# Twelve matmuls of a split-precision projection in another order: high by high, then the weight's low part, then the data's low part

## The reference

```python
qkv = x @ Wqkv + bqkv                      # 512 -> 3 * 512, split into q, k, v, 16 heads of 32
q_prime = exp(q @ omega - 0.5 * sum(q * q))    # 128 features a head; k_prime likewise
k_sum = sum over n of k_prime;  k_v = sum over n of k_prime (x) v
out = (q_prime @ k_v) / (q_prime @ k_sum + 1e-6)
x = layernorm(x + out @ Wout + bout)
x = layernorm(x + x @ weight.T + pooled(x) @ disha)
```

## Time and profile before

| | |
|---|---|
| runs, median (lowest to highest) | 2587.18 us (2584.82 to 2590.24), 3 runs |
| the profiled execution | 2590.89 us |
| its span | 2589.1 us |
| mean granted TensorE clock | 0.986 |
| busy: PE, PEld, DVE | 2439.8 us (94%), 1401.2 us (54%), 2010.7 us (78%) |
| busy: ACT, POOL | 1114.3 us (43%), 508.8 us (20%) |
| chain that ended last | PE 86%, DVE 7%, issue 2%, SPq 2%, ACT 2%, DMA 1% |

### The profile page before, as it was taken

One profiled execution on the slowest core, in us unless ns is written; L12 is line 12 of the kernel. 1 busy time (PEld: TensorE's weight loads), 2 busy tenths in 40 slices (PEclk: granted clock), 3 DMA queues, 4 the chain that ended last, 5 costly groups with the idle time before them and its releaser, 6 DMA issues.

```text
span 2589.1 us, 60402 instructions
## 1 busy us (share of the span) xinstructions
PE 2439.8 (94%) x24576; PEld 1401.2 (54%) x24576; DVE 2010.7 (78%) x3966; ACT 1114.3 (43%) x1921; POOL 508.8 (20%) x522
## 2 busy tenths in 40 slices
PE   5888999999999999999999999999999999987766
PEld 2445555555555555555555555555555555553333
DVE  5546878888888888888788888888888887876675
ACT  1444444444444444444445444444544444442221
POOL 2011121222212122221222222112222212211121
PEclk9999999999999999999999999999999999999998
DMA  5232233233223323322332333233223323312220
GB/s 168 67 83 56 87 92 94 67 93 100 73 81 92 95 70 95 96 75 79 96 91 76 87 96 83 71 100 88 78 85 96 92 64 99 88 54 58 58 58 33
DMA packets 158947, 214.49 MB, mean 83 GB/s; under 512 B 19312, under 2 KB 119760, under 8 KB 154448
## 3 DMA queue, kind: packets, MB, share of 16 engines
q1 hardware_dynamic: 158672, 210.63, 29.3%
HBM read 74.24 MB, written 33.55 MB: 42 GB/s over the span
## 4 chain that ended last, share of the span: by engine, by line
PE 86%; DVE 7%; issue 2%; SPq 2%; ACT 2%; DMA 1%; POOL 0%; DVEq 0%; POOLq 0%; ACTq 0%
PE bank_y L381 24%; PE bank_a L381 23%; PE bank_x L381 13%; PE bank_qf L464 4%; PE bank_kf L420 4%; PE bank_x L493 4%; PE kv_ps L438 2%; PE kv_ps L443 2%; PE bank_nm L482 2%; PE bank_nm L481 2%; PE bank_nm L480 2%; PE kv_ps L441 2%; DVE k_feat_lo L675 1%; SPq L304 1%; PE bank_x L391 1%
## 5 line engine op out<-in xcount | busy, mean ns | idle before, releaser
L792 POOL TENSOR_TENSOR rstd<-mean_var,minus_half 128x1 f32<-128x1 f32 x256 | 166.6, 651 | 1773.4 <-DVE mean_var L630 1773.4
L549 ACT ACTIVATE k_feat<-bank_kf 128x512 f32<-128x512 f32 x512 | 305.7, 597 | 232.5 <-PE bank_kf L420 220.9
L675 DVE TENSOR_TENSOR k_feat_lo<-k_feat 128x512 bf16<-128x512 f32 x512 | 358.5, 705 | 39.1 <-ACT k_feat L549 35.9
L558 ACT ACTIVATE q_feat<-bank_qf 128x512 f32<-128x512 f32 x512 | 305.5, 597 | 168.4 <-PE bank_qf L464 141.2
L682 DVE TENSOR_TENSOR q_feat_lo<-q_feat 128x512 bf16<-128x512 f32 x512 | 350.5, 694 | 33.1 <-ACT q_feat L558 29.9
L564 ACT ACTIVATE at_hi<-bank_x 128x512 f16<-128x512 f32 x128 | 76.4, 597 | 396.7 <-PE bank_x L493 396.7
L438 PE MATMUL kv_ps<-v_hi,k_feat 128*128 128x33 f16 x2048 | 208.8, 179 | 12.9 <-DVE k_feat_lo L675 9.0
L420 PE MATMUL bank_kf<-omega_s,stack_k 98*128 98x128 f16 x2048 | 199.9, 220 | 17.5 <-ACT k_feat L549 8.8
L464 PE MATMUL bank_qf<-stack_q,omega_s 98*128 98x256 f16 x1024 | 197.3, 274 | 15.2 <-ACT q_feat L558 15.2
L381 PE MATMUL bank_y<-wffn_hi,yt_hi 128*128 128x512 f16 x512 | 195.8, 382 | 16.2 <-DVE yt_lo L730 14.5
L381 PE MATMUL bank_y<-wout_hi,at_hi 128*128 128x512 f16 x512 | 195.6, 382 | 16.2 <-DVE at_lo L726 12.5
(11 more groups left out here) (118 smaller groups left out, 6076.2 us busy)
## 6 DMA issues: line engine op xcount, KB each, us to landing
xt_f<-xt SPq DMA_DIRECT2D x33, 1024.0 KB, 5.2
stack_k<-t_hi_k SPq DMA_DIRECT2D x256, 128.0 KB, 2.4
stack_q<-t_hi_q SPq DMA_DIRECT2D x256, 128.0 KB, 2.4
rows<-x SPq DMA_DIRECT2D x128, 256.0 KB, 2.9
out<-rows SPq DMA_DIRECT2D x128, 256.0 KB, 2.1
stack_k<-t_lo_k SPq DMA_DIRECT2D x128, 128.0 KB, 2.4
stack_q<-t_lo_q SPq DMA_DIRECT2D x128, 128.0 KB, 2.4
q_feat<-wqkv SPq DMA_DIRECT2D x2, 768.0 KB, 5.0
```

Of the source, the lines that this page charges most:

```text
L549: nc.scalar.activation(k_feat[:, i % 2, :], bank_kf[:, :], ACT.Exp, scale=1.0 / WS).then_inc(S["k_exp"], 1)
L558: nc.scalar.activation(q_feat[:, 2 * pair:2 * pair + 2, :], bank_qf[:, :].rearrange("p (e n) -> p e n", e=2), ACT.Exp, scale=1.0 / WS).the ...
L675: v.tensor_tensor(k_feat_lo[:, u, :], k_feat[:, u, :], k_feat_hi[:, u, :], ALU.subtract).then_inc(S["kfl"], 1)
```

## The change

`twelve` issues its matmuls by product and no longer by block: four high by high, four with the weight's low part, four with the data's low part. The halves are still six and six. The wait for the data's low part leaves the first half and stands at the ninth matmul (n == 8, the third of the last half). What KP0, WO and FF wait for in the first half is now the high part. VP, QP and the other KP had no such wait, and have one now at the ninth matmul.

```diff
-            def twelve(bank, parts, what, done):
-                at = [(kb, s, m) for kb in range(KB) for s, m in (("hi", "hi"), ("lo", "hi"), ("hi", "lo"))]
+            def twelve(bank, parts, what, done, order, low):
+                at = [(kb, *order[m]) for m in range(3) for kb in range(KB)]
                 for n in (range(0, 6) if what == "first" else range(6, 12)):
+                    if n == 8:
+                        wait(pe, *low)
                     lhs, rhs = parts(*at[n])
                     last = nc.tensor.matmul(bank[:, :], lhs, rhs, start=n == 0, stop=n == 11)
...
+            LHS_LOW_LAST = (("hi", "hi"), ("hi", "lo"), ("lo", "hi"))
+            RHS_LOW_LAST = (("hi", "hi"), ("lo", "hi"), ("hi", "lo"))
...
                         if i == 0:
-                            wait(pe, "xt_lo_done", kA + 1)
+                            wait(pe, "xt_hi_done", kA + 1)
                         bank_free(b, c, kind, i)
...
-                        wait(pe, "at_lo_done" if kind == "WO" else "yt_lo_done", TPC * j + i + 1)
+                        wait(pe, "at_hi_done" if kind == "WO" else "yt_hi_done", TPC * j + i + 1)
                         bank_free(b, c, kind, i)
                     l, r = (at_p, wo_p) if kind == "WO" else (yt_p[i % 2], wf_p)
                     twelve(bank_y, lambda kb, s, m: (l[s][:, kb, :], r[m][:, kb, :]), what,
-                           "wo_done" if kind == "WO" else "ff_done")
+                           "wo_done" if kind == "WO" else "ff_done", LHS_LOW_LAST,
+                           ("at_lo_done" if kind == "WO" else "yt_lo_done", TPC * j + i + 1))
```

More of the change, by code:

```diff
@@ L400, in step @@
                         if i == 0:
-                            wait(pe, "xt_lo_done", kA + 1)
+                            wait(pe, "xt_hi_done", kA + 1)
                         bank_free(b, c, kind, i)
                     twelve(bank_of(b, c, kind, i), lambda kb, s, m: (w3[s][:, kb, D + P * i:D + P * (i + 1)],
-                                                     xt_p[m][:, c % CPB, kb, :]), what, "kp_done")
+                                                     xt_p[m][:, c % CPB, kb, :]), what, "kp_done",
+                           RHS_LOW_LAST, ("xt_lo_done", kA + 1))
                 elif kind == "VP":
@@ L408, in step @@
                     twelve(bank_of(b, c, kind, i), lambda kb, s, m: (xt_p[s][:, c % CPB, kb, P * i:P * (i + 1)],
-                                                     w3[m][:, kb, 2 * D:3 * D]), what, "vp_done")
+                                                     w3[m][:, kb, 2 * D:3 * D]), what, "vp_done",
+                           LHS_LOW_LAST, ("xt_lo_done", kA + 1))
                 elif kind == "KN":
@@ L451, in step @@
                     twelve(bank_x, lambda kb, s, m: (w3[s][:, kb, P * i:P * (i + 1)],
-                                                     xt_p[m][:, (c + 1) % CPB, kb, :]), what, "qp_done")
+                                                     xt_p[m][:, (c + 1) % CPB, kb, :]), what, "qp_done",
+                           RHS_LOW_LAST, ("xt_lo_done", jq + 1))
                 elif kind == "QN":
```

## The result

The changed kernel takes 2573.46 us (median of 5 runs, 2568.61 to 2574.40) against 2587.18 us (5 runs, 2584.05 to 2591.00). The ratio is 0.9941, 95% interval 0.9925 to 0.9957: faster by 13.7 us by the medians, by 15.3 us by the ratio, where 2575 was forecast.

A forecast was written before the change was run, and what follows sets the result against it. TensorE was taken as the bound in the middle (busy 1987.48 of 2000 us), with idle time to win mainly at start and end. Terms 2.0 + 0.9 + 6.9 + 2.2 = 12.0 us off 2587.2 gave 2575.2, written 2575; range 2564 to 2583.5.

The forecast's parts named there:

- start: KP0's first eight matmuls run before xt_lo is ready, so KP2 and what follows move up: 2.0 us, bounds 0 and 3.4.
- six batch ends: Steady part: FF3 starts earlier, but NM then waits for DVE's division: 0.15 us each, 0.9 in all, bounds 0 and 8.7.
- four pairs: Last chunks: WO1's at_lo and FF0's yt_lo waits go, NM4 starts 1.72 us earlier per slot: 6.9 us, bounds 3.0 and 11.7.
- three single waits: Last chunks: 1.4 us at the last FF1, 0.4 at each of two WO3: 2.2 us together, bounds 0 and 6.5.
- satisfied waits: The waits added at the ninth matmul of all 640 projections, nearly all met long before, cost 0.
- order: Issuing the twelve matmuls of a projection in the new order costs nothing: 0.
- clock: WO1 and FF0 can have lost up to 4.9 us at 1.2 GHz; left out of the sum, put into the range.
- The clock follows: Rival: also, in two or three of the last slots WO1 and FF0 run at 2.4 GHz: 21 us less, 2566; chance 0.18.
- The wait only moves: Rival: pairs give as little as steady waits, only start and singles remain: about 3.5 us, 2583.7; chance 0.11.
- The ninth matmul pays: Rival: each projection's mid-stream wait costs a weight load's 0.10 us, 64 us less 12: 2639; chance 0.05.
- The clock falls more often: Rival: a pause inside the projection leaves WO1 and FF0 at 1.2 GHz in all four last slots: 2585; chance 0.04.

The follow-up runs named there:

- e4: Changed kernel, but WO and FF wait for the low part in their first half again; only KP0's wait has moved: 2589.40 us, ratio 0.9993 to the kernel before.
- e5: Changed kernel with GpSimd's first bias addition of a chunk moved from behind NM 0 to behind NM 1: 2569.21 us, ratio 0.9922 to the kernel before.
- e6: Kernel before the change, with only GpSimd's first bias addition moved from behind NM 0 to behind NM 1: 2592.00 us, ratio 1.0002.
- e9: Changed kernel, but WO waits for at_lo ahead of its first matmul again; FF and KP keep the new waits: 2576.60 us, ratio 0.9956.
- e2: Kernel before, old order and waits, plus an always-met wait for the low part at the ninth matmul of all 640 projections: 2591.27 us, ratio 1.0005.
- e1: Kernel before with the twelve matmuls in the new order, old waits at the first matmul and none at the ninth: 2589.34 us, ratio 0.9999.
- e10: e3 run a second time, beside the changed kernel on one chip: 2573.68 us, ratio 0.9941 to the kernel before.
- e3: Changed kernel, but KP0 waits for xt_lo ahead of its first matmul as before; only WO's and FF's waits have moved: 2572.41 us, ratio 0.9930.
- e8: The changed kernel run again, nothing altered, beside others on the same chip: 2572.44 us, ratio 0.9935 to the kernel before.
- e11: The changed kernel run a third time, nothing altered, as the measure for e9 and e10: 2570.76 us, ratio 0.9934 to the kernel before.
- e7: e5, and in the last chunks DVE makes yt_lo one place earlier (YT's lag 0, not 2): 2566.60 us, ratio 0.9907 to the kernel before.

## Why the prediction was right, and where it was off

The forecast of 2575.0 is 1.5 us above the median, and the waits move as predicted; one term, the batch ends, was mis-sized. That the time was hit so closely is in part luck. The forecast was a gain of 12.0 us, and the three comparisons of the changed kernel gave 13.7, 16.8 and 18.5 us by the medians, or 15.3, 16.8 and 17.1 by the ratios. And what the clock gave and took, which was left out, is far larger in its parts than in its sum. The terms, by the two profiled timelines, whose spans differ by 16.5 us:

| term | predicted us | from the timelines | what showed it |
| --- | --- | --- | --- |
| start | 2.0 | 2.04 | first KF; e4 has it too |
| six batch ends | 0.9 | 3.8 (about 2.5 in a typical execution) | NM at each end; e5, e6 |
| four pairs | 6.9 | 7.4 (4 x 1.86, at full clock) | NM to NM; e9 |
| three single waits | 2.2 | 2.06 (1.31, 0.35, 0.40) | AT2, QF behind WO3, YT2 |
| satisfied waits | 0 | 0 | e2 |
| order | 0 | 0 | e1 |
| clock | left out | about +1.1 | what the timelines have over; the parts are below |

**The start.** The size is right to 0.04 us in this pair of executions. Over all profiles the first KF starts at 51.68 to 52.63 us in the six kernels with the old wait (mean of 52.63, 52.01, 52.22, 52.54, 51.68 and 51.75: 52.1) and at 49.95 to 50.73 in the seven with the new one (50.4): 1.8 us, and no overlap. What follows is noisier than that. The clock between there and the first NM moves that NM by itself (10.7 us of low clock stand ahead of it in e10, 24.2 in before): it stands from 220.94 to 225.88 in the kernels with the old wait and from 221.12 to 223.79 in those with the new one, and the means, 224.1 and 222.7, are 1.4 us apart. Whether the start's gain reaches the end was not resolved by the times of e3, e4 and e10.

**The batch ends: the term that was mis-sized.** The step that failed is this one: "that needs the division L720, which ends at 530.46. DVE works there without a break behind the batch's closing of keys and values, and none of it waits for FF3. So NM starts at about 530.51". It took the durations of DVE's instructions as fixed, and one end as the pattern of all six. One of those instructions was long only by a collision. In the kernel before the rows behind the earlier trace rows are

```profile
528.07 1.62 DVE L751 TENSOR_SCALAR rows<-rows,mean_var,rstd 128x512 f32<-128x512 f32 x1
...
528.14 1.27 POOL L780 TENSOR_TENSOR rows<-rows,bias_out 128x512 f32<-128x512 f32 x1
```

while its median over 128 is 0.541. And two of the six ends before had no collision, here the third:

```profile
1130.08 0.55 DVE L751 TENSOR_SCALAR rows<-rows,mean_var,rstd 128x512 f32<-128x512 f32 x1
...
1130.69 1.26 POOL L780 TENSOR_TENSOR rows<-rows,bias_out 128x512 f32<-128x512 f32 x1 [0.64 <-DMA rows<-x]
...
1130.97 0.42 DVE L720 TENSOR_TENSOR attn<-bank_nm,den 128x256 f32<-128x256 f32 x1
...
1132.68 0.18 PE L480 MATMUL bank_nm<-kv_hi,q_feat 128*128 128x33 bf16 x1
```

There the division ends at 1131.39, 1.29 us ahead of NM, and the twelve matmuls of FF3, started late, hid it. Counted as the prediction counts, such an end is worth 1.24 us and the six together about 3, which the trace of before already held. After the change an end without the collision gives 1.1 to 1.2 us (4.28 - 3.15; 5.42 - 4.22), and one with it about what was predicted, 0.15 (from -0.06 to 0.22). Three good ends of six made 3.8. In the six profiled executions with the changed FF wait and the addition where it was (after, e8, e11, e3, e10, e9), 10 ends of 36 are good (3, 2, 2, 2, 1, 0), so that a typical execution has about 2.5 us from this term: 36 ends with 10 x 1.1 + 26 x 0.15 is 14.9 us, and a sixth of it 2.5. The change does not make the good ends more frequent, as far as so few can tell: with FF's old wait and the addition where it was (before, e1, e2, e4) 7 ends of 24 have a short instruction (2, 1, 2, 2). What it does is to let them count. In every good end, before and after, GpSimd's addition stood waiting for its rows' DMA. The median run gained 13.7 where these two profiled ones are 16.5 apart, and this is part of it; the rest was not followed up.

**The pairs.** 1.86 us in place of 1.72, between the same two NM where the clock is full in both kernels (18.28 and 18.29 us before, 16.44 and 16.43 after). Both steps of the argument are seen: WO1 starts at its bank (0.32 us behind the residual), and DVE's idle inside the pair closes; NM4 waits for q_feat_lo. e9 divides it in halves. The prediction had the upper end of the range at 2.92 a pair, if DVE kept up; it did not, and the other 1.1 us of the two waits are DVE's own work.

**The singles.** 1.31, 0.35 and 0.40 for 1.4, 0.4 and 0.4. At the last FF1, 2.36 us of wait became 1.15 in front of AT2. A wait that is removed turns into the next one on the same engine, and its price is the difference of the two.

**The waits added and the order.** Nothing, by e1 and e2, which bound them at 0.1 to 0.15%. In the profiled execution after, only two of the 640 waits at the ninth matmul were not met: 2.5 us for `xt_lo` at the start and 0.2 at one FF0.

**The clock.** Leaving it out of the sum did little harm, but only since its parts cancel. It did follow inside the pairs: in the last WO1 and FF0 of before the clock was 0.50, and the same instructions ran after at

```profile
2520.00:2525.00 5.00, 4.91 (x40) 2.73 (x38) 0.94 (x3) 0.60 (x1) 0.00 (x0) 0.70 0.03 11
2525.00:2530.00 5.00, 4.24 (x44) 2.57 (x44) 4.68 (x11) 1.42 (x3) 1.78 (x2) 1.00 0.00 0
2530.00:2535.00 5.00, 3.76 (x22) 2.05 (x22) 4.79 (x11) 2.19 (x5) 0.55 (x1) 1.00 0.44 136
2535.00:2540.00 5.00, 3.82 (x19) 1.35 (x17) 4.60 (x10) 2.14 (x4) 2.19 (x2) 1.00 0.07 26
```

with 2.4 GHz from 2525 on. That last pair gave 6.28 us (2533.09 to 2525.72 ahead of it is 7.37, 2556.00 to 2542.35 behind it 13.65), 4.4 more than the 1.86 of a pair, and the third gave 1.5 more. But in the stretch ahead, from 2520, the clock is 0.70, and in the first of the last chunks the QP at 2326.42 and the NM behind it ran at the low clock and cost 2.1 us that before did not pay. From place to place, what the distance between the timelines did beyond the terms of the table is +1.1 (50 to 60 us), -2.1, -2.5 (behind the first pair), +1.5, -1.7 and -0.8 (between the third pair and the last), +4.4 and +1.2 (behind AT2): together +1.1.

This repeats. I took the granted clock between the same two NM of each pair in all traces. With the old waits of both WO and FF (before, e1, e2, e4, e6) 13 of 20 pairs hold 3.4 to 10.2 us of low clock and take 19.75 to 22.90 us; the other seven take 18.28 or 18.29. With both new waits (after, e3, e5, e7, e8, e10, e11) none of 28 holds any, and they take 16.44 to 16.63, but for two of 17.18 and 17.43, where the ninth matmul waits 0.70 and 0.96 us for `yt_lo` (e3 and e8). So the clock does follow in the pairs: a kernel with the old waits spends 79.2 us in its four pairs in the mean, one with the new waits (without e7) 66.3, which is 13 us and not 7.4. But the stretches between the pairs are longer after, 138.0 us for the three in the mean and not 133.0, so that nearly all of the clock's gain is given back there. The low clock has moved, and has not become less: over 2240 to 2560 us, the granted clock is 0.94, 0.94, 0.95 and 0.93 in before, e1, e2 and e6, 0.93, 0.94, 0.94, 0.94, 0.94, 0.94 and 0.94 in after, e5, e7, e8, e9, e10 and e11, and 0.96 in e3 and e4. e3, with 0.96, had made up its late start by the end: its profiled span is 2572.5 us, that of after 2572.6. The rule of the Trainium skill (Perfetto Trace Analysis, "Matmul Optimizations"), that matmuls execute "back-to-back in batches", agrees with the pairs, which lose their idle time and their low clock together. Whether pauses at the ninth matmul cost clock was not tested, since only two or three of 640 occurred in an execution.

**The rivals.** *The clock follows*: true inside the pairs, given back between them. *The wait only moves*: it does in most batch ends (1.25 us at NM for 1.45 at FF3), but in the pairs it does not; e9 shows 0.93 a pair even with half the change. Its price was also added up wrongly: the start and the singles alone are 4.2 us and not 3.5, and with 0.15 us for each pair and each batch end 5.7, that is 2581.5 and not 2583.7. *The ninth matmul pays*: excluded by e2. *The clock falls more often*: it falls in none of the pairs' WO1 and FF0 after.

## What to carry to other kernels

Ordering a split product so that the operand that is made last is used last cost nothing measurable here and lets each projection start on the parts that are there; it pays where its engine idles for that part, and there by the difference to the next wait on the same engine, not by the wait it removes. Before you take an instruction's duration as fixed in such a count, hold it against the least and the median of all executions of the same line, and read every place to which the term applies: one that stands three times above them may be a collision that is absent in some places, or that can be moved away on purpose. A short one that earns nothing now can count once the wait that hid it is gone. And try the two edits together: moving the bias addition was worth nothing without the early start of FF3, and 3 us with it.

## What the runs showed of the hardware

- DVE's TENSOR_SCALAR of 128 x 512 f32 with one tensor input takes 0.54 us alone, and 1.48 to 1.65 us when GpSimd's TENSOR_TENSOR of the same size (1.26 to 1.27 us) gets ahead of it; it then ends 0.28 us behind GpSimd's end (826.53 after 826.24; 529.69 after 529.41). When DVE gets ahead, it keeps its 0.55 us and GpSimd's is drawn out, to 1.52 us in the changed kernel, and ends 1.12 us behind DVE's end (1728.16 after 1727.05).
- Which of the two is held can be told from the records' starts, with an offset. In the ten traces with the addition in its old place, this instruction of DVE is held whenever GpSimd's record starts between 0.07 us ahead of DVE's and 0.10 us behind it (528.07 and 528.14 in before; 827.22 and 827.31, with 1.65 us, in e11), and is never held from 0.13 us behind on (1730.52 and 1730.65 in e3). The Trainium skill (SBUF — State Buffer, "SBUF: two separate sides") describes a port pair that DVE's fast modes and GpSimd share as an "exclusive lock": who starts first has it for the whole instruction. Both cases agree with that, if GpSimd is taken to start some 0.1 us earlier, against DVE, than its record shows. Whether this instruction of DVE runs in such a mode no row shows, and it is not held for all of its work: it ends 0.28 us behind GpSimd's end, where it takes 0.54 alone.
- A satisfied semaphore wait in the middle of a stream of matmuls, 640 times, costs between -0.8 and 3.6 us in all (e2).
- Between 50 and 60 us, behind the start's thin stretch, the clock is low for a time that differs between executions of the same program: in two executions of the changed kernel (after and e8) the granted clock from 50 to 55 us is 0.68 and 0.50, from 55 to 60 it is 0.98 and 0.90. Before against after (0.65 and 0.67 against 0.68 and 0.98) this moves all that follows by 1.1 us.
- In the last chunks TensorE's low clock (1.2 GHz) left the pairs when their waits of 2.08 and 0.84 us went (13 of 20 pairs with the old waits hold some, none of 28 with the new ones), and came in other places instead: the granted clock from 2240 to 2560 us is 0.93 to 0.96 in either group.
